# A mixture-of-experts stage in blocks of 288 rows instead of 128, both layers with stationary weights and interleaved

## The reference

```python
gate_logits = jnp.einsum('bsh,eh->bse', x, gate_w)          # 8 experts
gate_probs = jax.nn.softmax(gate_logits, axis=-1)
top_v, top_i = jax.lax.top_k(gate_probs, TOP_K)             # 2 of 8 for each token
for e in range(E):
    h = jax.nn.silu(jnp.einsum('bsh,hf->bsf', x, w1[e]) + b1[e])     # 512 -> 2048
    y = jnp.einsum('bsf,fh->bsh', h, w2[e]) + b2[e]                  # 2048 -> 512
    out = out + y * comb_w[..., e:e + 1]
```

## Time and profile before

| | us |
|---|---|
| median of 3 runs | 1471.64 |
| lowest and highest | 1469.05, 1473.18 |
| span of the profiled execution | 1469.3 |
| TensorE busy | 1237.3 |
| VectorE busy | 1016.8 |
| ScalarE busy | 761.8 |

### The profile page before, as it was taken

One profiled execution on the slowest core, in us unless ns is written; L12 is line 12 of the kernel. 1 busy time (PEld: TensorE's weight loads), 2 busy tenths in 40 slices (PEclk: granted clock), 3 DMA queues, 4 the chain that ended last, 5 costly groups with the idle time before them and its releaser, 6 DMA issues.

```text
span 1469.3 us, 33539 instructions
## 1 busy us (share of the span) xinstructions
PE 1237.3 (84%) x12366; PEld 848.8 (58%) x12367; DVE 1016.8 (69%) x1663; ACT 761.8 (52%) x1227; POOL 298.5 (20%) x363
## 2 busy tenths in 40 slices
PE   3735799998588999847489999768999999999996
PEld 2205576775466677423345555636677677767674
DVE  3668888888788888869567667475567755476432
ACT  2236577677666767622643424424466655375331
POOL 0121223332222333422000000034111111111111
PEclk9766999999899999979599999658999999999998
DMA  4043000003200000320220000328347564446111
GB/s 147 1 155 123 13 5 5 5 3 115 69 12 6 5 4 4 104 119 11 97 115 0 0 0 0 134 107 254 136 143 250 191 201 136 143 168 219 24 26 22
DMA packets 38129, 120.26 MB, mean 82 GB/s; under 512 B 9960, under 2 KB 14184, under 8 KB 28080
## 3 DMA queue, kind: packets, MB, share of 16 engines
q1 hardware_dynamic: 32416, 107.28, 20.3%
q0 software_dynamic: 5648, 12.13, 4.1%
HBM read 105.61 MB, written 12.76 MB: 81 GB/s over the span
## 4 chain that ended last, share of the span: by engine, by line
PE 47%; DVE 4%; ACT 2%; issue 2%; POOL 0%; POOLq 0%; DVEq 0%; ACTq 0%
PE banks L2349 16%; PE banks L2370 15%; PE banks L1880 7%; PE banks L1910 3%; PE banks L2319 1%; PE banks L2302 1%; PE banks L1936 1%; PE banks L2336 1%; PE banks L1949 1%; ACT ab_wi_hi L1749 1%; PE banks L2295 1%; PE banks L1959 1%; DVE f_qa L1418 0%; PE banks L1933 0%; ACT ab_un L1783 0%
## 5 line engine op out<-in xcount | busy, mean ns | idle before, releaser
L2349 PE MATMUL banks<-eb_x_hi,eb_w_hi 128*128 128x128 f16 x1344 | 228.7, 220 | 4.7 <-DVE eb_w_lo L2229 4.7
L2349 PE MATMUL banks<-eb_x_lo,eb_w_hi 128*128 128x128 f16 x1344 | 228.6, 220 | 0.0
L2349 PE MATMUL banks<-eb_x_hi,eb_w_lo 128*128 128x128 f16 x1344 | 228.6, 220 | 0.0
L1118 PE MATMUL banks<-mb_u_hi,mb_wi_hi 128*128 (+3 forms) x1088 | 190.7, 221 | 12.4 <-ACT mb_ca L845 10.7
L1118 PE MATMUL banks<-mb_u_hi,mb_wi_lo 128*128 (+3 forms) x1088 | 190.4, 221 | 0.0
L1118 PE MATMUL banks<-mb_u_lo,mb_wi_hi 128*128 (+3 forms) x1088 | 190.2, 221 | 0.0
L2229 DVE TENSOR_TENSOR eb_w_lo<-eb_raw,eb_w_hi 128x2048 f32 (+1 forms) x64 | 142.6, 2287 | 23.0 <-ACT eb_w_hi L2235 16.0
L647 DVE SCALAR_TENSOR_TENSOR mb_ca<-mb_xp,mb_par,mb_ca 128x128 f32<-128x128 f32 x384 | 149.5, 451 | 5.2 <-ACT mb_ca L845 3.4
L2349 PEld LDWEIGHTS banks<-eb_x_hi,eb_w_hi 128*128 128x128 f16 x1344 | 132.4, 99 | 7.4 <-issue 5.1
L2349 PEld LDWEIGHTS banks<-eb_x_lo,eb_w_hi 128*128 128x128 f16 x1344 | 132.4, 98 | 2.4
L2349 PEld LDWEIGHTS banks<-eb_x_hi,eb_w_lo 128*128 128x128 f16 x1344 | 132.4, 99 | 0.0
(11 more groups left out here) (441 smaller groups left out, 2842.6 us busy)
## 6 DMA issues: line engine op xcount, KB each, us to landing
eb_raw<-e_w SPq DMA_DIRECT2D x64, 1024.0 KB, 6.0
mb_ring<-m_in_w SPq DMA_DIRECT2D x8, 1072.0 KB, 6.5
ab_raw<-a_in_w SPq DMA_DIRECT2D x4, 1154.0 KB, 9.0
mb_ring<-m_out_w SPq DMA_DIRECT2D x4, 1024.0 KB, 5.3
xcm<-x_cm SPq DMA_DIRECT2D x4, 512.0 KB, 5.1
t_res<-x_tm SPq DMA_DIRECT2D x1, 2048.0 KB, 8.9
t_kept<-t_res SPq DMA_DIRECT2D x8, 256.0 KB, 2.0
mb_wi_hi<-t_kept SPq DMA_DIRECT2D x1, 2048.0 KB, 9.2
```

Source lines behind the costliest of these rows:

```text
L1118: x = e.matmul(ps[0:width, bank, n * P:(n + 1) * P], a[:, k, f:f + width], b[:, k, ds(i * P, P)], start=(k == 0 and m == 0), stop=(k == KD ...
L2349: o = e.matmul(ps[:, j, c * P:(c + 1) * P], a[:, side, k, f * P:(f + 1) * P], b[:, k, :], start=(k == 0 and m == 0), stop=(k == KD - 1 and ...
```

## The change

- A block is 288 rows of one expert (`EX_B`), moved in three parts of 128, 128 and 32 (`SUBS`). Slots in the table, the plan's rounding and the reserve rows follow. A count above 288 makes a second block.
- Layer 1 as before with 288 columns, one group to a bank, two banks in turn. Layer 2 now keeps w2 in the array and streams h: y comes out turned (features by rows), in four banks.
- TensorE interleaves them (`layers`): layer 1 of group f, then layer 2 of group f - 2. The transposes of the next x stand between the last groups of layer 2; those of the block before's y (`turn_y`) between groups 2 and 4.
- ScalarE adds the bias in the activation and does SiLU twice, once to f32 and once to f16; no bias add is left on VectorE. The bias of the expert is first copied to `b1_now`.
- ScalarE and VectorE make one piece of the next expert's weights after every second group.
- y goes from PSUM to `yT` (`keep_y`, ScalarE and VectorE two parts each), is turned back in the next block, weighed (`weigh`) and sent (`deliver`) there.
- `sel16`, `marks`, `b2` and some small tiles move to room that is used at other times; `y` lies in `t`.

The core of the diff:

```diff
-BLOCKS = TOK // P
-
-FILLED = TOPK * TT + E + 1
-MOST = FILLED - 2
-LEAST = TOPK * TT
-TABLE = FILLED + BLOCKS
+
+EX_B = 288
+SUBS = tuple((q * P, min(P, EX_B - q * P)) for q in range(-(-EX_B // P)))
+NSUB = len(SUBS)
+BLOCKS = -(-TOK // EX_B)
+LEAST = -(-TOPK * TOK // EX_B)
+MOST = (TOPK * TOK + E * (EX_B - 1)) // EX_B
+FILLED = NSUB * (MOST + 3)
...
+EX_LAG = 2
+EX_RING = 4
...
+            def ahead(n):
+                if not last:
+                    pieces(x + 1, 1 - side, n, start)
+
+            with e.If(0 < count):
+                block(x, start + 0, ahead)
+            with e.Else():
+                for n in range(EX_PIECES):
+                    ahead(n)
+            with e.Fori(1, BLOCKS) as b:
                 with e.If(b < count):
-                    block(x, start + b, lambda: None)
+                    block(x, start + b, lambda n: None)
...
+        for k in range(1, BLOCKS):
+            own(e.scalar_tensor_tensor(out=nb[:], in0=before[:, TT, :], scalar=EX_B * k + 0.5, in1=nb[:],
+                                       op0=ALU.is_gt, op1=ALU.add))
...
+        own(e.memset(yT[:], 0.0))
+        e.sem_inc(yt_done, YT0)
+        for k in range(KD):
+            lower_x(e, 0, k)
...
-        def block(x, s, pieces):
-            for j in range(EX_FG):
-                bias(x, s, j)
-                if j:
-                    low(s, j - 1)
-            low(s, EX_FG - 1)
-            lower_x(e, s + 1)
...
+        def low(s, f):
+            e.wait_ge(hhi_done, s * EX_FB + (f + 1 + HHI0))
+            e.tensor_tensor(h_lo[:, f % EX_RING, :], hb[:, f % 2, :], h_hi[:, f % EX_RING, :], ALU.subtract)\
+                .then_inc(hlo_done, 1)
+
+        def weigh(s, q):
+
+            n = SUBS[q][1]
+            if q == 0:
+                e.wait_ge(y_sent, s + YSENT0)
+                e.wait_ge(who_in, 16)
+                e.wait_ge(t_sent, 16 * TT)
+            e.wait_ge(y_turned, s * NSUB + (q + 1))
+            core.apart(e)
+            e.tensor_scalar(y[0:n, q, :], ps[0:n, TURN_BANK + q % 2, :], who[0:n, ds(s * NSUB + q, 1), 1], None, ALU.mult)\
+                .then_inc(y_ev, 1)
+
+        def keep_y(s, d):
+
             e.wait_ge(y_mm, s + 1 + YMM0)
-            e.wait_ge(y_sent, s + YSENT0)
-            e.wait_ge(who_in, 16)
-            core.apart(e)
-            e.tensor_copy(row[:], who[:, ds(s, 1), 0])
-            e.tensor_scalar(y[:], ps[:, 5, :], who[:, ds(s, 1), 1], None, ALU.mult).then_inc(y_ev, 1)
-
-        def pieces(x, side, i, start):
-            for q in range(EX_RAWS):
-                lower(e, x, side, i * EX_RAWS + q, q)
+            e.tensor_copy(yT[:, d, :], ps[:, Y_BANK + d, 0:EX_B]).then_inc(yt_done, 1)
+
+        def block(x, s, ahead):
+            for f in range(EX_FB):
+                low(s, f)
+                if EX_LAG <= f < EX_LAG + NSUB:
+                    weigh(s, f - EX_LAG)
+                if f % 2:
+                    ahead(f // 2)
+            for k in range(KD):
+                lower_x(e, s + 1, k)
+            for d in (2, 3):
+                keep_y(s, d)
...
+        def activate(s, f):
+            rise = ps[:, H_BANK + f % 2, 0:EX_B]
+            e.wait_ge(h_mm, s * EX_FB + (f + 1))
+            e.wait_ge(hlo_done, s * EX_FB + (f + 1))
+            e.activation(hb[:, f % 2, :], rise, ACT.Silu, bias=b1_now[:, f:f + 1])
+            e.activation(h_hi[:, f % EX_RING, :], rise, ACT.Silu, bias=b1_now[:, f:f + 1]).then_inc(hhi_done, 1)
+
+        def keep_y(s, d):
+            e.wait_ge(y_mm, s + 1 + YMM0)
+            e.copy(yT[:, d, :], ps[:, Y_BANK + d, 0:EX_B]).then_inc(yt_done, 1)
+
+        def block(x, s, ahead):
+            e.activation(b1_now[:], b1[:, ds(x, 1), :].rearrange("p o c -> p (o c)"), ACT.Copy).then_inc(b1_done, 1)
+            e.wait_ge(b1_done, s + 1)
+            for f in range(EX_FB):
+                activate(s, f)
+                if f % 2:
+                    ahead(f // 2)
+            for k in range(KD):
+                upper_x(e, s + 1, k)
+            for d in (0, 1):
+                keep_y(s, d)
+
+        def pieces(x, side, n, start):
+            q = n % EX_RAWS
+            if n == 0:
+                e.wait_ge(y_mm, start + YMM0)
+            e.wait_ge(raw_in[q], x * (EX_PIECES // EX_RAWS * 16) + (n // EX_RAWS + 1) * 16)
+            e.copy(w_hi[:, side, n, :], raw[q]).then_inc(whi_done, 1)
...
+        def turn(s, k):
+
+            if k == 0:
+                e.wait_ge(xg_in, s * (NSUB * 16) + NSUB * 16)
+            if k >= 2:
+                e.wait_ge(xlo_done, s * KD + (k - 1))
             core.apart(e)
+            for q, (at, n) in enumerate(SUBS):
...
+        def turn_y(s, q):
+
+            at, n = SUBS[q]
+            if q == 0:
+                e.wait_ge(yt_done, s * KD + YT0)
+            if q >= 2:
+                e.wait_ge(y_ev, s * NSUB + (q - 1))
+            core.apart(e)
+            for d in range(KD):
+                x = e.transpose(ps[0:n, TURN_BANK + q % 2, d * P:(d + 1) * P], yT[:, d, at:at + n], core.ident[:])
+            x.then_inc(y_turned, 1)
+
+        for k in range(KD):
...
+        def layers(s, x, side):
+            for f in range(EX_FB):
+                layer1(s, side, f)
+                if f < EX_FB - 1 and f >= EX_LAG:
+                    if f < EX_LAG + NSUB:
+                        turn_y(s, f - EX_LAG)
+                    layer2(s, x, side, f - EX_LAG)
+            e.wait_ge(y_ev, s * NSUB + NSUB)
+            turn(s + 1, 0)
+            turn(s + 1, 1)
+            layer2(s, x, side, EX_FB - 3)
+            turn(s + 1, 2)
+            turn(s + 1, 3)
+            layer2(s, x, side, EX_FB - 2)
+            layer2(s, x, side, EX_FB - 1)
...
+        def fetch(s):
+
+            e.wait_ge(turned, s * KD)
+            core.apart(e)
+            e.tensor_copy(row_x[:], who[:, ds((s + 1) * NSUB, NSUB), 0]).then_inc(idx_done, 1)
+            e.wait_ge(idx_done, s)
+            core.apart(e)
+            for q, (_, n) in enumerate(SUBS):
+                gather(row_x[0:n, q:q + 1], q, n)
+
+        def deliver(s):
+
+            e.tensor_copy(row[:], who[:, ds(s * NSUB, NSUB), 0]).then_inc(row_done, 1)
+            e.wait_ge(row_done, s + 1)
+            for q, (_, n) in enumerate(SUBS):
+                e.wait_ge(y_ev, s * NSUB + (q + 1))
+                core.apart(e)
+                e.indirect_dma_start(out=core.out, out_offset=bass.IndirectOffsetOnAxis(ap=row[0:n, q:q + 1], axis=0),
+                                     in_=y[0:n, q, :], in_offset=None, compute_op=ALU.add).then_inc(y_out, 16)
+
+        fetch(1)
 
         def block(s):
-            e.wait_ge(turned, s + 2)
-            core.apart(e)
-            e.tensor_copy(row_x[:], who[:, ds(s + 2, 1), 0]).then_inc(idx_done, 1)
-            e.wait_ge(idx_done, s + 1)
-            core.apart(e)
-            gather(row_x[:, 0:1])
-            e.wait_ge(y_ev, s + 1 + YEV0)
-            core.apart(e)
-            e.indirect_dma_start(out=core.out, out_offset=bass.IndirectOffsetOnAxis(ap=row[:, 0:1], axis=0),
-                                 in_=y[:], in_offset=None, compute_op=ALU.add).then_inc(y_out, 16)
-            e.wait_ge(y_out, s * 16 + 16)
+            deliver(s)
+            fetch(s + 2)
...
+        deliver(total)
...
```

More of the change, by code:

```diff
@@ new lines, in stage_moe @@
+    hb = sb("hb", [P, 2, EX_B])
+    h_hi, h_lo = sb("h_hi", [P, EX_RING, EX_B], F16), sb("h_lo", [P, EX_RING, EX_B], F16)
+    yT = sb("yT", [P, KD, EX_B])
+    turned_x = yT[:].rearrange("p k n -> p (k n)")[:, 0:2 * D].rearrange("p (b f) -> p b f", b=2)
+    y = t[:, 0:NSUB, :]
+    mine, who = sb("mine", [P, TOPK * TT, 2]), sb("who", [P, TABLE, 2])
+    row, row_x = sb("row", [P, NSUB], U32), sb("row_x", [P, NSUB], U32)
+    tok16, rows = sb("tok16", [P, TT], F16), sb("rows", [P, NSUB], U32)
@@ L2116, in dve @@
         for n in range(len(EX_FIRST_AT)):
-            lower(e, 0, 0, n, n)
+            lower(e, 0, 0, n)
         wide = lambda x: x.unsqueeze(2).to_broadcast([P, TT, E])
@@ L2223, in dve, with lower @@
+        def pieces(x, side, n, start):
+            lower(e, x, side, n)
         e.wait_ge(plan_done, 1)
         experts(e, pieces, block)
-    def lower(e, x, side, n, q):
+        total = e.value_load(plan[0:1, 2 * E:2 * E + 1], min_val=LEAST, max_val=MOST)
+        for q in range(NSUB):
+            weigh(total, q)
+    def lower(e, x, side, n):
         e.wait_ge(whi_done, x * EX_PIECES + (n + 1))
-        e.tensor_tensor(w_lo[:, side, n, :], raw[q], w_hi[:, side, n, :], ALU.subtract).then_inc(wlo_done, 1)
@@ L2231, in upper @@
[L2231 to L2244 removed]
+        e.tensor_tensor(w_lo[:, side, n, :], raw[n % EX_RAWS], w_hi[:, side, n, :], ALU.subtract).then_inc(wlo_done, 1)
@@ L2246, in act, with lower_x, upper_x @@
+    def lower_x(e, s, k):
+        e.wait_ge(xhi_done, s * KD + (k + 1))
+        e.tensor_tensor(x_lo[:, k, :], ps[:, TURN_BANK + k % 2, 0:EX_B], x_hi[:, k, :], ALU.subtract).then_inc(xlo_done, 1)
+    def upper_x(e, s, k):
```

(46 more changed lines are left out.)

224 lines of the change are left out of this document (89 added, 135 removed).

## The result

The changed kernel takes 1524.57 us (median of 4 runs, 1523.78 to 1528.19); beside it the kernel before took 1472.41. The ratio is 1.0368, 95% interval 1.0348 to 1.0389: 3.7% slower. The forecast was 1532, in a range of 1490 to 1565.

The account below looks back on a forecast made before the run. TensorE bounds the expert stage. Stage start 989.1, TensorE work 395.7, first-block wait with clock (2.7 + 21.5 + 2.3), new code 4, seven boundaries 88.9 and end 25.5 give a 1529.7 us span, forecast 1532, range 1490 to 1565.

Parts of the forecast that it names:

- first matmul at: Start of the expert stage: TensorE's first matmul comes about 3 us later than 986.05, at 989.1 us.
- TensorE's work at full clock: Eight blocks of matmuls (122.5 ns each) and transposes (up to 110 ns each): 395.7 us, 56.2 less than before.
- idle: first block: First block: VectorE waits for the table `who`, holding up TensorE, 21.5 us idle (15 to 28).
- idle: the x waits: Block ends: TensorE's third x transpose waits for `lower_x`, behind ScalarE's cast and VectorE's `lower`; 3.9 us, seven times.
- idle: blocks' starts: Block starts: TensorE waits for ScalarE's SiLU behind y, skipped rounds and two table loads; 4.2 us, seven times.
- low clock: After idle gaps TensorE runs at 1.2 GHz for a while: 2.3 us lost each return, twice a block.
- code met first: Code run for the first time in the stage adds 4 us.
- end: After the last matmul: skipped rounds, y transposes, weighing and transfers take 25.5 us instead of 14.05.
- What would show it: Expected trace signs, including about 4 us idle in each block's third group, released by ScalarE's SiLU, seven times.
- The rival of the code: Longer loops no longer stay on chip, so jumps fetch code: about 4 us more each boundary, 1560 us; 17%.
- The rival that it stays high: The clock stays high over the boundary gaps: 15 x 2.3 us less, about 1497; 8%.
- The boundaries are cheap: Boundaries between blocks cost under 4.1 us each, so the kernel is faster: 1443 to 1471 us; 10%.

Follow-up runs that it names:

- experiment 10: Experiment 8's kernel with one TensorE body instead of two, the weights' side a register in the matmuls' addresses: 1427.41 us, ratio 0.9714.
- experiment 1: Changed kernel with the next expert's last weight piece cast and lowered behind the passes over the next x, not ahead: 1498.23 us, ratio 1.0184.
- (6): Changed kernel with TensorE's eight blocks written out, no loop and no branch over the side: 1523.04 us.
- (7): Changed kernel with the eight experts written out on ScalarE and VectorE, no loops and no branch on the count: 1504.92 us, ratio 1.024.
- experiment 8: Changed kernel with weight pieces moved earlier, y turned back late, SiLU first, y kept at the next block's start, skipped loops branched around: 1449.33 us, ratio 0.9851.
- 9: Experiment 8's kernel with TensorE's eight blocks written out, no loop and no branch: 1428.86 us, ratio 0.9714.
- (11): Experiment 10's kernel with one body for both sides on ScalarE too: 1421.33 us, ratio 0.9665.
- experiment 4: Changed kernel with 48 extra matmuls of 128 columns filling TensorE's x wait at each block's end: 1514.13 us, ratio 1.0292.
- Experiment 3: Changed kernel with y of the block before turned back, weighed and delivered in rounds 12 to 14, not 2 to 4: 1506.97 us, ratio 1.0242.

## Why the prediction was right

The sum, term by term (us):

| term | predicted | measured |
|---|---|---|
| first matmul at | 989.1 | 989.8 |
| TensorE's work at full clock | 395.7 | 404.8 (8 x 50.60, experiment 10) |
| idle: first block | 21.5 | 19.7 (17.84 and 1.84) |
| idle: the x waits | 7 x 3.9 = 27.3 | 7 x 3.04 = 21.3 |
| idle: blocks' starts | 7 x 4.2 = 29.4 | 30.4 |
| low clock | 37.2 | 33.4 (what is left) |
| code met first | 4 | none apart from the idle time |
| end | 25.5 | 24.1 |
| span | 1529.7 | 1523.5 |

The mechanism was mostly right, and the sum is nearer than its terms: TensorE's work was set 9 us too low, and the x waits, the code met first and the low clock 14 us too high together. That they cancel is luck.

- *TensorE's work.* The straight line between 128 and 512 columns gave 122.5 ns, which is what the trace shows, and 115.8 at 272. The matmuls were right; the transposes were set too low: six of x take 0.94 us (157 ns each), not 110 ns each. With 0.44 us for four of y, a block has 3.2 us of transposes and not 2.4: 6.4 of the 9 us. The rest is at the first matmuls behind the transposes, where twelve take 1.58 us and not 1.47, and at a block's start (36 in 4.58, not 4.41).
- *The end of a block.* Place, releaser and mechanism were right (experiment 1). The wait is 0.9 us shorter, since two SiLUs overlap (0.9, not 1.0), the two passes of `lower_x` follow closely, and TensorE's slower transposes cover more.
- *The start of a block.* The size was right, the cause only in part, and so its agreement (29.4 and 30.4) is partly luck. ScalarE's chain is the bound: taking TensorE's gaps away gained nothing (6), taking ScalarE's chain away gained 19.7 us (7). But I gave all seven to SiLU, in the third group of the block. The trace has that wait alone at three (blocks 3, 5 and 7), behind a gap of TensorE's own at two (2 and 4), and not at all at two (1 and 6). ScalarE's jump back held 3 us more at blocks 2 and 4. "What would show it" was wrong on this point.
- *The rival of the code.* It came true as a mechanism and not at its price. Experiments 8 to 11 show that a loop of two bodies stalls at the jump back from the second (gaps of 4.2 to 4.6 us on TensorE, about 3 on ScalarE), and that a loop of one body does not. It added little here because the two stalls lay under each other and under the table loads. I had given it 4 us at every boundary; TensorE pays it at every second one, and once at block 1. "Runtime: NRT & Kernel Launch", section "Instruction fetch mechanics", in the Trainium skill describes a stall at a taken branch to a page not on the chip, and calls the cost in straight code mostly hidden. Experiments 6, 9 and 10 agree.
- *The clock.* Shown by experiment 4 for the x wait. The size was about right: 2.6 us behind 3.84 us of idleness at block 7 and 1.8 behind the x wait ahead of it, 4.4 against 4.6. The mean over seven is 4.1: the 33.4 less 4.4 in the first block, worked out from its 32 slow matmuls and slow transposes. But it is not a sum over gaps (7). The rival that it stays high is refuted.
- *The table.* Experiment 3 gives back 17.6 us. The read took 8.16 us within my bounds of 6.7 to 14.5, and started 0.8 us earlier than I had it. I had it wait for the writes of `out`; in the code and on the chain it waits for GpSimd's 16 row transfers (`told`). The last of these took 8.53 us to land. The queues moved 319 GB/s then, weights and the writes of `out`, so the writes can still have a part; it was not tried. That other traffic matters is likely: the same read took 8.2 us beside 35 GB/s here and 13.8 beside 253 GB/s in experiment 8.
- *The boundaries are cheap*: refuted at 11.5 us each (3.04 + 4.34 + 4.1), against the 4.1 that decides. But the same work with cheap boundaries is faster than before, by 3.3% with 288 rows (11). The 47 us less work on TensorE were real; boundaries, table and end had spent more than twice that.
